# One adaLN transformer layer on one core: rotation of q and k on another vector engine, first loads and instruction order changed

## The reference, cut to what matters

```python
mod = (silu(c) @ wmod).reshape(4, 6, 1, -1)           # sa, ca, ga, sb, cb, gb
h = layernorm(x) * (1 + ca) + sa
q = rope(heads(h @ Wq + bq, 16)); k = rope(heads(h @ Wk + bk, 4)); v = heads(h @ Wv + bv, 4)
att = softmax(causal(q @ k.T / 4))                    # head size 16, 4 query heads per key head
x = x + ga * (merge(att @ v) @ Wo + bo)
h = layernorm(x) * (1 + cb) + sb
x = x + gb * ffn(h)                                   # a routed block: rmsnorm, two products, rmsnorm, gated MLP of 704
# rope(x): x1, x2 = x[..., 0::2], x[..., 1::2]; concat([x1*cos - x2*sin, x1*sin + x2*cos])
```

## Time and profile before

| | |
|---|---|
| median of 3 runs | 486.77 us (486.62 to 486.94) |
| the profiled execution's own time | 489.17 us |
| its span, first to last instruction | 487.4 us |
| TensorE busy in it | 444.7 us (91%) |
| VectorE, ScalarE, GpSimd busy | 338.9, 281.7, 225.8 us |
| mean granted TensorE clock | 0.983 |

### The profile page before, as it was taken

The page is one execution under the profiler, slowest core; times in us unless marked ns, Lnnn a source line. Parts: engine busy times, 40 slices in busy tenths (PEclk is TensorE's granted clock), DMA queues, the critical chain, the costliest instruction groups (busy, mean ns, idle before and its releaser), DMA issues.

```text
span 487.4 us, 9404 instructions
## 1 busy us (share of the span) xinstructions
PE 444.7 (91%) x3320; PEld 372.3 (76%) x3320; DVE 338.9 (70%) x745; ACT 281.7 (58%) x574; POOL 225.8 (46%) x297
## 2 busy tenths in 40 slices
PE   2687699979999999899999999989999999999994
PEld 2275355677678589778766999879889779999994
DVE  3569968488988337998873688898687635376552
ACT  1183657676559757345487763526857488454440
POOL 5382946621283421331747506275261744348244
PEclk9997989998999999999999999999999999999998
DMA  7904020000000000020020100010001001001011
GB/s 201 300 1 137 2 88 1 1 2 5 3 1 24 1 1 2 1 86 8 3 88 1 34 2 1 5 44 3 1 33 48 1 1 45 1 2 45 1 43 44
DMA packets 16448, 16.04 MB, mean 33 GB/s; under 512 B 4105, under 2 KB 14798, under 8 KB 16402
## 3 DMA queue, kind: packets, MB, share of 16 engines
q1 hardware_dynamic: 16402, 15.43, 10.0%
...
## 4 chain that ended last, share of the span: by engine, by line
PE 80%; DVE 6%; ACT 5%; issue 3%; DMA 2%; SPq 2%; POOL 1%; POOLq 0%; ACTq 0%; DVEq 0%
PE banks L784 8%; PE banks L785 8%; PE banks L786 8%; PE banks L701 8%; PE banks L713 7%; PE banks L675 7%; PE banks L574 5%; PE banks L654 5%; PE banks L575 5%; PE banks L576 5%; PE banks L738 3%; PE banks L664 2%; DMA wm_st<-in_L_wmod 2%; DVE stk L1124 2%; ACT QKT L890 2%
## 5 line engine op out<-in xcount | busy, mean ns | idle before, releaser
L784 PE MATMUL banks<-gTh,guhi 128*128 128x256 f32 x352 | 101.7, 289 | 1.6 <-DVE mx L1139 1.5
L785 PE MATMUL banks<-gTl,guhi 128*128 128x256 f32 x352 | 98.1, 279 | 0.0
L786 PE MATMUL banks<-gTh,gulo 128*128 128x256 f32 x352 | 98.1, 279 | 0.0
L910 ACT ACTIVATE PT<-banks 128x1024 f32<-128x1024 f32 (+3 forms) x96 | 74.4, 809 | 29.0 <-PE banks L701 24.2
L1139 DVE TENSOR_REDUCE mxp<-banks 128x2 f32<-128x1024 f32 (+3 forms) x56 | 62.2, 1142 | 12.1 <-PE banks L675 6.7
L784 PEld LDWEIGHTS banks<-gTh,guhi 128*128 128x128 f32 x352 | 66.5, 189 | 4.2 <-issue 3.5
L785 PEld LDWEIGHTS banks<-gTl,guhi 128*128 128x128 f32 x352 | 66.4, 189 | 0.5
L786 PEld LDWEIGHTS banks<-gTh,gulo 128*128 128x128 f32 x352 | 66.4, 189 | 0.0
L675 PE MATMUL banks<-QKT 128*128 128x512 f32 (+3 forms) x192 | 53.4, 384 | 13.3 <-ACT QKT L890 5.0
L701 PE MATMUL banks<-QKT 128*128 128x512 f32 (+3 forms) x192 | 52.2, 374 | 3.0 <-DMA QKT<-mrT 1.9
L537 POOL TENSOR_SCALAR_AFFINE_SELECT PT<-PT 128x512 f32<-128x512 f32 x32 | 20.7, 647 | 67.6 <-ACT PT L910 67.6
...
## 6 DMA issues: line engine op xcount, KB each, us to landing
...
```

The source lines that it names most:

```text
L784: pe.matmul(out_, guhi[:, k, blk, :], gh, start=(m == 0 and k == 0), stop=False)
L785: pe.matmul(out_, guhi[:, k, blk, :], gl, start=False, stop=False)
L786: i = pe.matmul(out_, gulo[:, k, blk, :], gh, start=False, stop=(m == len(blocks) - 1 and k == KB - 1))
L910: act.activation(PT[:, u % 2, 2 * q:2 * q + 2, 0:CH - q0], both("prob", b, n)[:, :, 0:CH - q0], ACT.Exp, scale=float(D) ** -0.5).then_inc( ...
```

## The change

`rope` and `stlo` leave VectorE's queue and join GpSimd's, with the same operands, the same shapes and the same waits. The first loads are issued in another order: x first, then Wq, Wk, Wv, then the first columns of wmod. The weights and the biases of q, k and v get semaphores of their own, and the bias part of `setw` and `asetw` becomes the steps `setb` and `asetb`. ORDER is written anew from the first word to the last.

```diff
-DVE_STEPS = dict(..., qkvb=NJ, rope=NC, stlo=NC, mxr=NM, ...)
-POOL_STEPS = dict(rstd1=NC, norm1=NT, pmask=ND, ...)
+DVE_STEPS = dict(..., qkvb=NJ, mxr=NM, ...)
+POOL_STEPS = dict(rstd1=NC, norm1=NT, rope=NC, stlo=NC, pmask=ND, ...)
...
-            sp.dma_start(wm_st[:, :, 0:CH], wmod[:, 0:CH]...).then_inc(l_modc, 16)
             load_x(0, 0)
             sp.dma_start(wq_st[:], ...); sp.dma_start(wk_st[:], ...); sp.dma_start(wv_st[:], ...)   # l_qkv
-            sp.dma_start(bb_st[:, 0:C], ...).then_inc(l_qkv, 16)        # and two more
+            sp.dma_start(wm_st[:, :, 0:CH], wmod[:, 0:CH]...).then_inc(l_modc, 16)
+            sp.dma_start(bb_st[:, 0:C], ...).then_inc(l_bias, 16)       # and two more
             load_x(0, 1)
...
+                elif kind == "rope":            # on GpSimd, waits as before
+                    for m, (u, v) in enumerate(((ev, cs), (od, sn), (ev, sn), (od, cs))):
+                        i = pool.tensor_tensor(rt[:, m], u, v, ALU.mult)
+                    then(i)
+                    pool.tensor_tensor(rot[:, :, :, 0:HALF], rt[:, 0], rt[:, 1], ALU.subtract)
+                    pool.tensor_tensor(rot[:, :, :, HALF:D], rt[:, 2], rt[:, 3], ALU.add).then_inc(S["rope"], 1)
+                elif kind == "stlo":            # on GpSimd: two subtractions into stk
```

More of the change, by code:

```diff
@@ L104 @@
 ORDER = """
[L105 to L158, removed]
-a4 a6 gate1 rs1 sum route route up4 gate6 ms2 hmod sil fft sum ms2 rs2 ms1 hT7 h2 hhi hlo gate5 h2 ffhi sil h2T1 h2hi
@@ L160 @@
-h2lo fft sil ffhi fin a7 up6 a0 rs1 fflo fft ffl route route up1 up4 gate5 gate7 gate0 up6 sil ffhi ms2 fflo fft ms2
-rs2 sil fft down1 sum h2 h2 h2T7 down4 h2hi h2lo sum gate7 gate1 gate4 up5 up3 sil sil ffhi ffhi fflo fft fin ffl ffhi
-sil fflo fft down2 ffhi fft ffhi fflo sum up3 sil fft ffhi fflo down2 ffl down3 down4 sum sum sum fin fin store store
-store
+ldx ldx stats rstd1 norm1 pzero norm1 xT4 setw vkeys norm1 norm1 stats rstd1 norm1 pmodc xT5 norm1 norm1 norm1 vmodc
+setb asetw asetb xev wts qkv4 bias6 xT7 pmod amod xev gmod ldx ldG ldB ldx ldW biasq pprep0 xT6 qkv5 xev afwv qkvb
@@ new lines @@
+qkvb aprep qkv7 xev qkv3 wts rope qkvb qkvb aprep sthi aprep pprep1 aw1 stlo stack4 stack6 rope stk stk sthi stlo
+stats rstd1 norm1 norm1 norm1 gprep gprep max4 mxr max0 mxr max6 mxr max2 max0 max6 mxr norm1 stack2 stack4 stk stk
+aprep mxr mxr mneg max6 mxr max0 max4 max6 mtT2 mrow max2 gprep gprep mxr mxr mxr max4 mxr mxr max2 max0 awd gwd max6
+max4 mxr mxr mrd prob2 mxr mxr max0 prob6 prob4 exp exp max2 prob6 exp mxr max0 max4 mxr mxr mxr mneg stats pmask exp
+pmask pv6 prob2 prob0 pv gw1 exp prob2 exp pmask exp prob4 exp mtT0 mrow pmask pv pv ycopy bias7 yT6 ytm wob ldx stats
@@ new lines @@
+rstd1 xT1 norm1 norm1 rstd1 ynT6 xT0 ynev wo6 xev biasq mrd prob4 exp ldx prob2 ldG norm1 exp wo7 prob4 prob2 exp x1
+x1 pv1 prob4 prob6 exp exp prob2 pv exp exp prob4 exp pv rstd2 norm2 rstd2 norm1 hmod norm2 hmod prob2 exp prob6 exp
+hT5 qkv4 prob2 pv prob6 xev hhi hlo stats pmask qkv0 xT5 pv ms1 exp exp xev prob6 ms1 rs1 a5 route prob2 pmask pv
+norm1 norm1 exp exp prob6 exp prob2 a5 route rs1 xT6 pmask pv exp pmask ms2 ms2 rs2 pv qkvb qkvb hT2 hhi rope ycopy
+qkv7 yT1 hlo ytm a5 a2 route route h2 h2 xev h2T3 h2hi h2lo ynT4 qkv6 ms2 sthi ynev gate5 qkvb qkvb wo4 x1 wts ms2
@@ new lines @@
+norm1 stlo stack6 stack0 stk stk max6 mxr max2 max0 up4 mxr mxr sil max6 max0 fft wo5 max2 ldW rs2 rope h2 sthi h2
+h2T4 rstd2 stlo mxr mxr stack6 stk stack0 norm1 mxr mneg mtT3 mrow h2hi mrd max6 max2 x1 rstd2 mxr mxr h2lo norm2 hmod
+stk gate5 sil max6 max0 max2 prob4 mxr mxr mxr gate6 prob0 rstd1 exp max4 prob2 exp exp norm2 ms1 max0 prob2 mxr mxr
+max4 pmask pv7 exp max0 max2 mxr mxr prob4 pmask pv prob0 exp exp max4 mxr max2 mxr prob0 exp pmask pv prob0 exp ffhi
+max4 mxr mxr max0 mxr wob hT2 hhi up3 up5 bias4 xT0 pmask pv hlo sil ycopy xev mneg a1 mtT2 yT7 gate0 hmod ms1 mrow
@@ new lines @@
+sil gate3 yT2 h2T0 h2hi sil hT1 hhi sthi up5 stlo ytm norm2 hmod fft hlo gate3 sil ffhi fft h2lo qkvb fflo gate1 sil
+qkv2 qkvb stack4 up6 fft ffhi up0 fflo fft stk max2 stack4 rope ynT6 mxr ffhi ffhi fflo down1 sum stk sthi max2 max4
+max0 ynev mxr mxr up7 max2 max4 mxr mxr gate6 mxr mneg stlo stack2 ffl sil fft wts down4 stk max0 max6 ffhi sum gate5
+mxr mxr max0 mxr sil max2 max6 max4 mtT0 up1 mxr mxr mxr fflo stack6 wo2 x1 down3 sum fin store ldx stk mrow max4 max6
+mxr max2 gate0 fft a4 mxr mxr up1 sil fft max6 mxr wo5 mrd prob2 x1 down0 sum max6 max0 ffhi ffhi exp ms1 prob2 ffl
@@ new lines @@
+rstd2 fflo down5 exp fin route mxr mxr prob2 stats exp prob6 exp pmask pv4 prob2 prob0 exp exp max6 max2 pmask pv
+prob0 exp pmask pv prob0 mxr exp a6 hT7 hhi rstd1 norm1 rs1 mxr mneg pmask bias2 ms2 route mtT3 mrow down0 pv norm1
+sum hlo sum ms2 a5 xT3 ycopy yT4 fin norm1 rstd2 rs2 xev a0 ytm ynT3 ynev biasq route ldW wob route mrd prob6 exp
+prob2 exp wo5 x1 prob6 wo4 prob0 prob2 pv5 rstd2 ms2 h2 exp h2 exp exp prob6 pv prob0 ms2 x1 exp exp prob2 h2T4 qkv6
+prob0 pv rs2 h2 h2 exp h2T2 norm1 xT7 exp h2hi store ldx stats pv prob0 xev norm2 h2lo h2hi h2lo qkv7 rstd1 norm1
@@ new lines @@
+norm1 xT4 norm1 norm1 exp pmask xev rstd2 prob0 exp prob2 exp pmask qkv4 xT1 xev prob2 pv prob0 pv exp exp norm2 prob2
+prob0 exp exp hmod ms1 gate3 sil pmask up0 pv hT2 hhi pmask pv up3 hlo qkvb qkvb fft hmod rs1 a2 gate6 ycopy route
+rope sil ms2 ms1 ffhi fft gate0 a7 gate5 route fflo hT6 ffhi sil qkvb yT2 ytm sil sthi up1 up7 ynT5 qkv3 fft hhi ms2
+ffl stlo stack0 hlo fft ffhi ffhi gate2 fflo qkvb rs2 h2 h2 h2T3 stk ynev sil up4 fft norm2 stack6 rope rs1 max0 max4
+wo2 mxr mxr stk max0 max6 h2hi down4 h2lo x1 ffhi mxr gate3 wo2 up5 max0 fflo sum mxr sthi stlo stack6 ldB sil fft stk
@@ L164 @@
+h2lo gate7 up5 gate1 sil fft sil ffhi up3 sum fft ffhi gate5 sil fflo up4 fft ffhi fin store fflo ffl down3 sum down4
+sum down2 sum fin fin store store store
 """.split()
@@ L1042, in _ @@
                                                   AX.X, ALU.add)
-                    assert setup(i) == V_SETW
+                    assert setup(i) == (V_SETW if kind == "setw" else V_SETB)
                 elif kind == "vkeys":
```

124 lines of the change are left out of this document (75 added, 49 removed).

## The result

The changed kernel took 490.21 us (median of 8 runs, 489.27 to 492.87), the kernel before 486.95 us beside it (8 runs, 484.96 to 489.21). The ratio is 1.0054, 95% interval 1.0033 to 1.0076: slower, by 2.6 us by the ratio and 3.3 us by the medians. The forecast was 490.8 us and 4.0 us slower.

What follows compares the result with a forecast made beforehand. A start bounded by a chain of latencies, then 418 us with TensorE nearly full. 489.17 + 7.5 (start) - 3.5 (relief) = 493.2 us, carried to the median: 490.8 us; range 483.5 to 498, likeliest case 488 to 495.

Steps and rivals of the forecast that it cites:

- VectorE's relief: Behind the first `prob`, TensorE's 6.5 us of waits on VectorE shrink: 3.5 us gained, bounds zero and 13.8 us.
- step 1: At the start, x no longer shares the queue with wmod: it lands at 6.5 us, `stats` 1.4 us earlier.
- (2): At the start, `pzero` (3.2 us) lies between two `norm1`; the second ends at 14.5 us and `xT.0.0` waits.
- (3): At the start, `pmodc` behind `xT.0.0` runs from 15.0 to 18.6 us; `qkv.0.0` starts at about 20.2 us.
- (4): `pmod`, now behind `qkv.0.0`, `bias` and `xT.0.2`, runs from 23.1 to 28.9 us; second pair goes through at 32.3.
- (5): `gmod`, 10.0 us, stands ahead of `rope.0.0` on GpSimd: rotation starts at 40.1 us, `stack` at 47.3 and 56.5.
- (6): Behind the second `stack` pair part is won back: first `prob` at 67.9 us, 7.5 us later, pure TensorE idle time.
- The loads pay: Rival at the start: `xT.0.0` not waiting behind `pzero` returns 3.2 us, 487.6 us; no chance of its own given.
- The upper bound of 1.31 us: Highest cost of one moved instruction on GpSimd, against 0.71 us taken; a chunk's chain would be 12.2 us.
- The steady part: Behind the first item, TensorE work of 10 us or more covers each chunk's 7.1 us chain: nothing charged, 3.5 us gained.
- the sign named for relief: In the changed kernel, waits of TensorE behind `mxr` come to below 3 us in total.
- GpSimd and VectorE holding each other: Part of a rival (495 to 505 us, chance 0.18): `rope` holds VectorE up to 4.3 us, giving 497 us.

Runs made afterwards that it cites:

- the second profile of the old order: Profile, 487.20 us, of the kernel before with the new order of the first loads alone; median 487.96 us, ratio 1.0008.
- e3_later_items: The kernel before, old order and old loads, with `rope` and `stlo` on GpSimd for items 1 to 3 only: 492.04 us, ratio 1.0103.
- e5_gmod_vector: The changed kernel with the six instructions of `gmod` moved to VectorE, behind the second `qkvb`: 484.86 us, ratio 0.9931 to the kernel before.

## Why the prediction was right, and where its reasons were wrong

The sign and the size came out: +2.6 to +3.3 us for +4.0. The start went as reasoned. The gain in the steady part was put at about half its size, and put down to VectorE's relief alone, which no run shows by itself. Against the second profile of the old order the start cost 8.4 us, where 7.5 had been said, and the rest gave 6.1 for 3.5, so the total is nearer than its parts, and that is luck.

The start, step by step (starts in us, from the traces):

| | predicted | measured | before |
|---|---|---|---|
| x lands (step 1) | 6.5 | 5.7 | 7.9 |
| first `xT`, behind `pzero` (2) | 14.5 | 13.6 | 21.9, behind `pmod` |
| `pmodc` (3) | 15.0 | 14.5 | 6.6 |
| first `qkv` (3) | 20.2 | 19.3 | 23.4 |
| `pmod`, start and length (4) | 23.1, 5.85 | 23.0, 3.60 | 16.1, 5.85 |
| second `qkv` ends (4) | 32.3 | 29.9 | 27.3 |
| first rotation, behind `gmod` (5) | 40.1 | 37.5 | 28.1 |
| `stack`, first and second (5) | 47.3, 56.5 | 44.5, 55.5 | 34.3, 45.8 |
| first `prob` (6) | 67.9 | 67.7 | 60.4 |

- **Steps 1 to 3** held within 1 us: x landed 0.8 us earlier than taken.
- **Step 4, mis-sized.** `pmod` was charged 5.85 us and took 3.60. The 5.85 us came from a stretch that had mostly run at TensorE's lower clock level; in the changed kernel `pmod` stands behind it (see the last section). The rest of the step is right: `pmod` behind `qkv`, `amod` ahead of `xev`, so that the second pair waits.
- **Step 5, right, and shown by taking it away.** `gmod` took 9.7 us (10.0 said) ahead of the rotation. With `gmod` off GpSimd, `prob` came 7.5 us earlier in the profiled execution, and the median fell by 5.4.
- **Steps 5 and 6, mis-sized the other way.** The two `stack` pairs were charged 1.9 us each and took 3.65 and 3.34, at the lower granted clock. That is 1.7 and 1.4 us too little. Of the 2.8 us in hand at the first `stack`, 1.0 was left at the second and 0.2 at `prob`: the 67.9 was met by errors that cancelled.
- **"The loads pay".** They do, by 2.4 us in the trace of the new order and by nothing in the old one (1.0008). The rival's 3.2 us for `pzero` came to 2.0 alone.
- **The instructions.** 0.73 us for 0.71; 48.63 less 1.93 of clearing is 46.7 us on GpSimd for 46. The upper bound of 1.31 us was met by none; the longest took 1.20. VectorE was said to come to 307 us and came to 312.4: 26.5 us were freed, which is the undisturbed price, and not the 32.0 of the earlier trace rows. Of the 5 us or so of held-up time nothing was freed; which instructions now bear it the runs do not settle.
- **The steady part, the step that failed.** The prediction charged nothing for the longer chain, "this cover is 10 us or more", and credited 3.5 us to "VectorE's relief". The runs separate the two. In the old order the longer chain costs 4 to 5 us net of any relief (`e3_later_items`), through ScalarE's and VectorE's queues, which the count of TensorE's cover left out. In the new order with the rotation on VectorE the part is 16 us longer than before. Only both together give 6 to 7 us back. Of these, 2.8 us are waits that VectorE ended (6.5 us before, 3.7 after), near the 3.5 that had been credited; 1.8 us are waits that ScalarE ended, which had been given nothing. TensorE's busy time in this part is 1.4 us less as well: before the change it has two stretches at a granted clock of 0.50 behind the first `prob` (61.7 to 65.1 and 109.5 to 112.9 us), after it none. Even the place that the prediction called the tightest, 6.3 us of work against 7.1, was covered: between the first and the second `stack` of item 1 9.7 us passed, without a wait at either. TensorE's waits behind maxima, 1.4 and twice 0.3 us, are 2.0 us in total, below the 3 that were said, so the sign named for relief is there; but it comes with an order written for this placement. How much a list written anew for VectorE would bring by itself was not tried and stays open.
- **GpSimd and VectorE holding each other** did not show as a chain: in the changed kernel the medians are undisturbed. It shows where both are dense, in `e5_gmod_vector`: beside `gmod` on VectorE the first rotation's products took 0.90 to 1.17 us instead of 0.71, which cost that rotation 1.7 us (30.53 to 36.4 us, against 4.2 us in the changed kernel).
